# Spreading the next batch's keys and V over the four softmaxes of a latents' attention, with the first products of the following perceptron in the last one

## The reference, cut to what matters

```
h = concatenate([ctx, latents])            # 375 + 112 rows per batch
q = latents @ q_w + q_b                    # 16 heads of 32
k, v = split(h @ kv_w + kv_b)
a = softmax(mask(q k^T / 32))
y = (a v) @ out_w + out_b + latents        # "project"
z = rmsnorm(y, postnorm_w)                 # turned back for the perceptron
out = gelu(z @ mlp_w1 + b1) @ mlp_w2 + b2 + latents   # hidden width 2048
```

## Time and profile before

| | |
|---|---|
| median of 3 runs | 3318.3 us (3316.11 to 3318.38) |
| the profiled execution's own time | 3324.42 us |
| its span | 3323.1 us |
| TensorE busy | 3102.3 us, 93% |
| VectorE, ScalarE, GpSimd busy | 41%, 34%, 30% |
| stage of the latents, from its first logits to the perceptron's first matmul | 2589.2 to 2990.8 us |
| perceptron behind it | 2990.8 to 3158.8 us |

### The profile page before, as it was taken

One profiled execution on the slowest core, in us unless ns is written; L12 is line 12 of the kernel. 1 busy time (PEld: TensorE's weight loads), 2 busy tenths in 40 slices (PEclk: granted clock), 3 DMA queues, 4 the chain that ended last, 5 costly groups with the idle time before them and its releaser, 6 DMA issues.

```text
span 3323.1 us, 43816 instructions
## 1 busy us (share of the span) xinstructions
PE 3102.3 (93%) x16648; PEld 2589.2 (78%) x16648; DVE 1353.3 (41%) x3056; ACT 1115.1 (34%) x2492; POOL 1004.4 (30%) x938
## 2 busy tenths in 40 slices
PE   6988888999999999999999999999899989979988
PEld 3555556888888888889888888888688777758866
DVE  5784866333333333433333333334211455541133
ACT  2333335333222222332232222323333444443331
POOL 4564544222122121231121211212352232335410
PEclk8897989999999999999999999999899999979989
DMA  6554631332122121121121221211111101101132
GB/s 216 180 169 165 197 127 51 140 128 104 61 84 82 69 88 69 66 85 59 69 101 67 77 82 69 88 69 51 38 64 62 40 24 40 42 28 67 51 93 79
DMA packets 95095, 285.93 MB, mean 86 GB/s; under 512 B 8280, under 2 KB 52824, under 8 KB 86056
## 3 DMA queue, kind: packets, MB, share of 16 engines
q1 hardware_dynamic: 94408, 282.44, 24.9%
q10 hardware_dynamic: 480, 0.69, 0.1%
HBM read 260.94 MB, written 22.15 MB: 85 GB/s over the span
## 4 chain that ended last, share of the span: by engine, by line
PE 73%; DVE 7%; ACT 6%; POOL 6%; issue 4%; DMA 3%; SPq 0%; POOLq 0%; ACTq 0%; DVEq 0%
PE bank L179 21%; PE bank L180 20%; PE bank L181 20%; PE bank L1789 5%; POOL W_lo L219 3%; PE bank L1774 2%; DMA W_raw<-in_weights 1%; ACT W_hi L210 1%; DVE max L1982 1%; PE bank L2356 1%; DMA v_spread<-v_rows 1%; ACT prob L1871 1%; ACT prob L2467 1%; PE bank L633 1%; POOL y L1213 1%
## 5 line engine op out<-in xcount | busy, mean ns | idle before, releaser
L2063 POOL TENSOR_SCALAR prob<-prob,inverse 112x376 f32<-112x376 f32 x256 | 144.2, 584 | 1285.6 <-DVE inverse L1988 1285.6
L219 POOL TENSOR_TENSOR W_lo<-W_raw,W_hi 128x1024 fp32r<-128x1024 f32 x138 | 329.5, 2410 | 147.6 <-ACT W_hi L210 144.1
L179 PE MATMUL bank<-ctx_hi,W_hi 128*128 128x376 f32 x1024 | 353.2, 345 | 4.3 <-DVE K_lo L261 2.8
L180 PE MATMUL bank<-ctx_lo,W_hi 128*128 128x376 f32 x1024 | 343.0, 335 | 0.0
L181 PE MATMUL bank<-ctx_hi,W_lo 128*128 128x376 f32 x1024 | 342.4, 334 | 0.0
L261 DVE SCALAR_TENSOR_TENSOR K_lo<-bank,vectors,K_hi 128x375 fp32r<-128x375 f32 (+1 forms) x288 | 172.9, 606 | 413.3 <-ACT K_hi L252 413.3
L179 PE MATMUL bank<-act_hi,W_hi 128*128 128x448 f32 x800 | 319.5, 399 | 11.9 <-DVEq L338 5.6
L180 PE MATMUL bank<-act_lo,W_hi 128*128 128x448 f32 x800 | 299.1, 374 | 0.0
L181 PE MATMUL bank<-act_hi,W_lo 128*128 128x448 f32 x800 | 298.6, 373 | 0.0
L1935 DVE TENSOR_TENSOR V<-bank,bv 128x512 f32<-128x512 f32 x168 | 116.2, 692 | 437.6 <-PE bank L1789 236.6
L1871 ACT ACTIVATE prob<-bank,minus 112x376 f32<-112x376 f32 x256 | 143.6, 573 | 433.4 <-DVE minus L1985 433.4
(11 more groups left out here) (256 smaller groups left out, 6417.1 us busy)
## 6 DMA issues: line engine op xcount, KB each, us to landing
W_raw<-in_weights SPq DMA_DIRECT2D x69, 1024.0 KB, 4.9
ctx_hi<-ctx_split SPq DMA_DIRECT2D x64, 752.0 KB, 4.3
ctx_lo<-ctx_split SPq DMA_DIRECT2D x64, 752.0 KB, 5.8
v_spread<-v_rows SPq DMA_DIRECT2D x128, 224.0 KB
att<-in_ctxT SPq DMA_DIRECT2D x16, 376.0 KB, 5.2
ctx_split<-W_hi SPq DMA_DIRECT2D x16, 376.0 KB, 3.8
ctx_split<-W_lo SPq DMA_DIRECT2D x16, 376.0 KB, 4.7
W_hi<-ctx_split SPq DMA_DIRECT2D x32, 188.0 KB, 4.0
```

What stands on the lines that cost most here:

```text
L179: nc.tensor.matmul(dst, left[0], right[0], start=first, stop=False)
L180: nc.tensor.matmul(dst, left[0], right[1], start=False, stop=False)
L219: pool.tensor_tensor(k.Wl[:, slot, cs, :], k.Wraw[:, cs, :], k.Wh[:, slot, cs, :].bitcast(F32), ALU.subtract).then_inc(*k.w_low.now((n, i)))
L2063: pool.tensor_scalar(k.Pm[:, h, :], k.Pm[:, h, :], k.rsum[:, h:h + 1], 1.0, ALU.mult, ALU.mult).then_inc(*k.prob_done.now((n, h)))
```

## The change

The list of logit_steps is written anew. In the first softmax of a batch now stand V of the latents (values b, 3) and the project of the batch before; in each group o stand the keys (b+1, o), the attend and the values (b+1, o) for o = 0 to 2. V of batch 0 for j = 0 to 2 is made ahead of the loop. The scaling of the normalised result becomes a step of its own ("scale") after the second group's logits, and the turn stands in the group 1. In the last batch, which has no next one, the hidden products of the perceptron's group 0 for the first four batches stand between attend 2 and the turns of group 3, and pe_mlp leaves them out; so that their banks are 4 to 7, the second perceptron's rotation of banks begins there. The context's last reader is now keys (b-1, 3), for which sp_context2 waits.

```diff
+def pe_hidden(k, tag, g, half):
+    pe, w, cols = k.nc.tensor, mlp_weight(tag, g), half_columns(half)
+    if g == 0 and tag == "2":
+        pe.wait_ge(*k.h2_low[half * HB + HB - 1])
+    for o in range(C):
...
 def pe_mlp(k, tag):
...
+        if g or tag == "1":
+            pe_hidden(k, tag, g, 0)
+        pe_hidden(k, tag, g, 1)
...
-    k.banks.rotate(keys, list(range(8)))
+    k.banks.rotate(keys, {"1": [0, 1, 2, 3, 4, 5, 6, 7], "2": [4, 5, 6, 7, 0, 1, 2, 3]}[tag])
...
 def logit_steps(b):
     nxt, prv = b + 1 < B, b > 0
-    steps = [("logits", b, 0, (0, 1, 2, 3))] + [("values", b, j) for j in range(3)]
-    steps += [("turns", b, 0, (0, 1)), ("logits", b, 1, (0, 1)), ("turns", b, 0, (2, 3)), ("values", b, 3),
-              ("logits", b, 1, (2, 3)), ("attend", b, 0)]
+    steps = [("logits", b, 0, (0, 1, 2, 3)), ("values", b, 3)]
     steps += [("project", b - 1)] if prv else []
-    steps += [("turns", b, 1, (0, 1)), ("logits", b, 2, (0, 1)), ("turns", b, 1, (2, 3)), ("logits", b, 2, (2, 3))]
-    steps += [("keys", b + 1, 0)] if nxt else []
-    steps += [("attend", b, 1)]
...
+    steps += [("turns", b, 0, (0, 1)), ("logits", b, 1, (0, 1)), ("turns", b, 0, (2, 3)), ("logits", b, 1, (2, 3))]
+    steps += [("scale", b - 1)] if prv else []
+    for o in range(C):
+        steps += [("keys", b + 1, o)] if nxt else []
+        steps += [("turn", b - 1)] if prv and o == 1 else []
+        steps += [("attend", b, o)]
+        if o == C - 1:
+            break
+        steps += [("values", b + 1, o)] if nxt else [("perceptron",)] if o == C - 2 else []
+        steps += [("latent keys", b + 1)] if nxt and o == C - 2 else []
+        if o + 2 < C:
+            steps += [("turns", b, o + 1, (0, 1)), ("logits", b, o + 2, (0, 1)), ("turns", b, o + 1, (2, 3)),
+                      ("logits", b, o + 2, (2, 3))]
+        else:
+            steps += [("turns", b, o + 1, (0, 1)), ("turns", b, o + 1, (2, 3))]
...
-    sp.wait_ge(*k.banks.filled(("v2", b - 1, 2) if b else ("q2", 1, C - 1)))
+    sp.wait_ge(*k.banks.filled(("k2", b - 1, C - 1) if b > 1 else ("v2", 0, 2) if b else ("q2", 1, C - 1)))
```

More of the change, by code:

```diff
@@ L2143, in mlp_weight @@
     return (W_M1 if tag == "1" else W_M2) + 2 * g
+def pe_hidden(k, tag, g, half):
[3 more added lines that the diff above has]
+    for o in range(C):
+        key = ("h" + tag, g, half, o)
+        pe.wait_ge(*k.banks.free(key))
+        for c in range(C):
+            m = mm3(k.nc, k.banks.tile(key)[:, 0:HALF], weight(k, w, c, o * P, P),
+                    (k.Hh[:, c, cols], k.Hl[:, c, cols]), c == 0, c == C - 1)
+        m.then_inc(*k.banks.filling(key))
 def pe_mlp(k, tag):
@@ L2256, in plan_latents @@
     keys = [("lt", b) for b in range(B)] + [("q2", half, o) for half in range(2) for o in range(C)]
-    keys += [("kl", 0, o) for o in range(C)] + [("k2", 0, o) for o in range(C)]
+    keys += [("kl", 0, o) for o in range(C)] + [("k2", 0, o) for o in range(C)] + [("v2", 0, j) for j in range(3)]
     at = {}
@@ L2284, in plan_latents @@
         u.use(key, 4 + key[3])
-    k.w_last[W_P] = ("v2", B - 1, 2)
+    k.w_last[W_P] = ("k2", B - 1, C - 1)
     k.w_last[W_P + 1] = ("k2", B - 1, C - 1)
@@ L2397, in pe_latents @@
     pe_need_weight(k, W_P + 2)
+    for j in range(3):
+        pe_values2(k, 0, j)
     for b in range(B):
@@ L2416, in pe_latents @@
                 pe_turn(k, ("nt", *which), k.Z)
+            elif what == "perceptron":
+                pe_need_weight(k, W_M2)
+                pe_hidden(k, "2", 0, 0)
     pe_project_out(k, B - 1)
@@ L2518, in act_latents @@
     act_queries2(k, 0)
+    for j in range(3):
+        act_values2(k, 0, j)
     for b in range(B):
@@ L2589, in dve_project_out, with dve_scale_out @@
     dve_moments(k, [k.Z[:]], ("post", b), square=True)
+def dve_scale_out(k, b):
+    dve = k.nc.vector
     dve.wait_ge(*k.root_done["post", b])
@@ L2619, in dve_latents @@
                 dve_project_out(k, *which)
+            elif what == "scale":
+                dve_scale_out(k, *which)
             elif what == "keys":
@@ L2625, in dve_latents @@
     dve_project_out(k, B - 1)
+    dve_scale_out(k, B - 1)
 def pool_latent_keys(k, b):
```

## The result

The changed kernel takes 3272.8 us (median of 4 runs, 3268.6 to 3277.9) against 3317.7 before: 44.9 us faster, ratio 0.986 (95% interval 0.9848 to 0.9873). The forecast was 3268, with a range of 3254 to 3290. Its profiled execution took 3268.6 us with a span of 3267.3.

What follows compares the result with a forecast made beforehand. TensorE, busy 93% of the span, was taken as the bound, so only its waits and slow time could be won. Gains 37.6 + 2.8 + 0 + 9.8 = 50.2 us: 3324.4 to 3274.2, less 6.1: 3268.1; range 3254 to 3290.

Steps and rivals of the forecast that it cites:

- 40.0 + 0.9 + 0.1 = 41.0: Ordinary batch on TensorE: 40.0 us work, 0.9 wait before group 1's head 1, 0.1 attend held by the copy.
- Batches 1 to 6: Six batches at 41.0 us plus 9.8 for latent keys: 255.8 against 293.4, gain 37.6 us.
- The clock: New batches: no clock loss taken, as the 0.9 us wait is shorter than the 1.15 behind which it stayed 1.00.
- 3 of lost clock: Old batch of 47.3 us: some 40 us of work, 4.2 of waits and 3 lost to low clock.
- the clock falls as today: Rival: clock falls behind the remaining wait in batches, 6 x 3 = 18 us, giving 3286; chance 0.09.
- The DMA rival: Rival: context loads late before keys 0; free up to 11.0 us, sign turns above 19.4, 3328 at 21; chance 0.03.
- Batch 0: Three values ahead of its logits, where TensorE waits 2.37 us: batch 1 begins at 2633.3, gain 2.8 us.
- The last batch: Last batch with tail: project still 49.0 us after its logits, perceptron's 48 matmuls taken as 11.8 us; gain 0.
- The perceptron's stage: Perceptron stage starts without 48 matmuls: gain 9.8 us, with the halving of the first four tiles covered.
- rivals with half the gain: Softmax chain takes TensorE's place, batch 44.0 us (chance 0.14), or clock falls (0.09); each 18 us less gain, 3286.
- with no gain: Rival: TensorE's waits reappear in full in group 1's block, 8 us per batch, giving 3318; chance 0.04.
- the slower one: Rival: context comes late, TensorE waits for a DMA before keys 0; 3328 at 21 us; chance 0.03.

Runs made afterwards that it cites:

- early keys: Kernel with the pieces moved, plus K_hi of keys 0 made ahead of group 1's exponentials and K_lo between maxima and inverses: 3258.1 us, ratio 0.9824.
- scaling put back: Changed kernel with the normalised result's scaling back at the end of the project's step on VectorE, waiting for GpSimd's power: 3279.7 us, ratio 0.9887.
- the pieces moved: Changed kernel with perceptron tile 0 ahead of turns 3, tiles 1 and 2 behind the last project, tile 3 behind the last turn: 3263.2 us, ratio 0.9842.

## Why the prediction was right

- **The account of a batch held.** "40.0 + 0.9 + 0.1 = 41.0" came out as 41.2: the work is 40.4 (early keys), since a group's keys, attend and values take 6.08 us at their new places (2677.71 to 2683.79) instead of the 5.87 worked out, and the wait is 0.5 to 0.6 instead of 0.9. The two nearly cancel. Batches 1 to 6 gave 36.3 us of the 37.6 against the same profile of before, 33.2 against the other profile of the old order. The scaling put back shows that group 1's chain on VectorE is where the batch is tight.
- **The clock** stayed at 1.00, as taken from the row behind a single wait, but this is no rule: behind batch 0's single wait of 1.34 to 1.41 us it fell in one of ten profiles, and behind one of 1.53 us before keys 0 it fell too. The prediction's "3 of lost clock" per batch was too much. Batches with the same waits at full clock are 1.5 us shorter, since a wait of 1.00 before keys 3 takes the rest. The forecast time doesn't hang on it, being added up from work and waits. In the new order no later wait takes a fall back: the one in batch 0 with the scaling back cost 3.0 us, so the rival "the clock falls as today" kept its price.
- **The DMA rival** was priced rightly: no wait as the change stands (the second load lands some 3.2 us before keys 0 need it, 3.8 forecast), waits of 3.3 to 3.8 us per batch when the loads are held back by 7.5.
- **Batch 0** was forecast 1.0 us too fast: the same 0.2 us more in each of three groups, and its first block takes 3.83 us (2592.55 to 2596.38) instead of 3.48.
- **The last batch** was forecast 0 and gave 1.1, since the 48 matmuls took 10.5 us there and not 11.8; by the tail of 61.4 us in another profile it gave nothing. The perceptron's stage was forecast 9.8 and gave 9.5. These two terms stand side by side in the sum, and that hides what they are: the same 48 matmuls, moved. The prediction charged 11.8 us for them in the one and credited 9.8 in the other, and didn't say that the step is then worth next to nothing. Measured by taking it out, it is worth 1.6 to 3.4 us; alone, 1.3.
- **The whole:** 48.0 us between the same rows against 50.2 forecast, 44.9 by the first medians, 41.6 and 44.2 by the two later ones. That the medians give 3 to 6 us less than the rows fits with the old order's profile, which was a slow execution with the clock below 1.00 in all six batches. The forecast took its gain from that profile and its start from the median of the runs; by an estimate from the two profiles (293.5 and 290.4 us) that is up to 3 of the 4.7 us by which it was too low (3268.1 against 3272.8). The rivals with half the gain, with no gain, and the slower one fell.

The version with the tiles at the waits and the early keys takes 3258.1 us, 58.1 under before and 14.0 under the changed kernel beside it (3272.0).

## What to carry to other kernels

Where one engine's order is written by hand and a second chain runs beside it, write down for each gap the time at which the chain lets the engine go on, and give each gap just enough independent work; 8.4 us of filler in a gap of 5.3 is lost in three other gaps. Work that is moved out of a full stage is worth only the wait that it fills where it lands, so cut it into pieces of the size of the waits. The name on a wait can be the wrong engine: a bank that is drained late hid behind GpSimd's name here, and moving the two small operations that drain it showed which it was. And one profile of a kernel isn't its typical execution: the same order gave batches of 47.5 and of 46.0 us.

## What the runs showed that was not expected

- The same wait of 1.41 us in batch 0 left the clock at 1.00 in the changed kernel's profile and was followed by 0.92 over batch 0 in the one with the scaling back, which costs 3.0 us (42.3 against 39.3) there.
- The same pair of waits of 1.7 and 1.37 us in the old order was followed by a batch at 0.93 or at 1.00, and the batches differ by 1.5 us only.
- The time up to the first changed line varied by 8.7 us between profiles of kernels that are the same up to there. A difference of spans must be taken between rows.
- The perceptron's stage got 1.8 us shorter with the pieces moved, where TensorE enters it behind a wait of 0.76 us instead of 3.2, at full clock instead of half.
